# Macaron block (feed-forward, selective scan, feed-forward) on one core: the hidden units of the feed-forward kept in full precision in one buffer, and two projection weights in one buffer that is reloaded in every chunk

## The reference, cut to what matters

```python
x = L0_attn_resid                                   # (4, 1024, 512) float32
x = x + 0.5 * ffn(layernorm(x), W_up, W_gate, W_down)
x = x + attn(layernorm(x), ...)                     # a selective scan, below
x = x + 0.5 * ffn(layernorm(x), W_up, W_gate, W_down)

def ffn(x, W_up, W_gate, W_down):                   # D = 512, F = 2048
    wu, wg, wd = ternary(W_up), ternary(W_gate), ternary(W_down)   # clip(round(w / s), -1, 1) * s
    return (silu(x @ wu.T) * (x @ wg.T)) @ wd.T

def attn(r, ...):                                   # E = 1024, N = 16 states
    rn = rmsnorm(r) * norm_w
    x = silu(causal_conv4(rn @ W_in) + conv_b)
    delta = softplus(x @ W_delta_1 @ W_delta_2 + b_delta_2)
    # per position: h = h * exp(delta * A) + (delta * x) * B;  y = sum over n of h_n * C_n
    return r + ((y + x * W_D) * silu(rn @ W_skip)) @ W_out
```

## Time and profile before

| what | value |
|---|---|
| time, three runs | 2798.93, 2801.0 (median), 2805.9 us |
| span of the profiled execution, from the first to the last instruction | 2796.2 us |
| span against the median of the runs | 4.8 us less |
| busy: PE, DVE, POOL, ACT | 93%, 88%, 85%, 67% of the span |
| granted TensorE clock, mean | 0.979 of full |

### The profile page before, as it was taken

One profiled execution on the slowest core, in us unless ns is written; L12 is line 12 of the kernel. 1 busy time (PEld: TensorE's weight loads), 2 busy tenths in 40 slices (PEclk: granted clock), 3 DMA queues, 4 the chain that ended last, 5 costly groups with the idle time before them and its releaser, 6 DMA issues.

```text
span 2796.2 us, 51718 instructions
## 1 busy us (share of the span) xinstructions
PE 2614.3 (93%) x17439; PEld 2021.6 (72%) x17439; DVE 2447.7 (88%) x3221; ACT 1879.0 (67%) x4340; POOL 2382.1 (85%) x2023
## 2 busy tenths in 40 slices
PE   5776899999999999999999999999999999999878
PEld 4555677777878777786777778677777877776655
DVE  4378899999999999899999999899999999999892
ACT  7374867676676767667676766767676676767651
POOL 1168899999898999999998999999999898999881
PEclk9898999999999999999999999999999999999989
DMA  7013222223222322222232222222222222222220
GB/s 274 31 55 72 60 61 76 56 58 83 59 74 60 80 50 65 77 63 73 58 81 53 70 69 63 73 63 75 54 72 66 66 69 65 73 57 68 64 55 8
DMA packets 94446, 192.44 MB, mean 69 GB/s; under 512 B 12588, under 2 KB 32232, under 8 KB 93672
## 3 DMA queue, kind: packets, MB, share of 16 engines
q0 software_dynamic: 20304, 73.93, 13.7%
q1 hardware_dynamic: 73880, 115.21, 13.0%
HBM read 106.26 MB, written 8.91 MB: 41 GB/s over the span
## 4 chain that ended last, share of the span: by engine, by line
POOL 41%; PE 32%; issue 12%; DVE 7%; ACT 2%; DMA 1%; POOLq 1%; DVEq 0%; ACTq 0%
POOL h L778 22%; PE ps L1596 10%; POOL h L795 7%; PE ps L1607 6%; PE ps L1619 6%; POOL hl L884 4%; PE ps L1553 4%; PE ps L1668 4%; DVE h L1342 3%; POOL u L892 2%; POOL delta L849 2%; DVE xc L1400 1%; PE ps L1629 1%; POOL h L784 1%; POOL xw L799 1%
## 5 line engine op out<-in xcount | busy, mean ns | idle before, releaser
L778 POOL TENSOR_TENSOR h<-u,bb 128x1024 f32<-128x1024 f32 x512 | 1257.8, 2466 | 27.2 <-DVE u L1417 14.2
L1342 DVE TENSOR_TENSOR_SCAN h<-ps,h 128x512 f32<-128x512 f32 x1024 | 1191.8, 1207 | 36.5 <-POOL h L784 18.6
L1037 ACT ACTIVATE ps<-delta,a_neg 128x255 f32<-128x255 f32 x2048 | 873.1, 468 | 377.0 <-DVE h L1342 374.8
L1596 PE MATMUL ps<-xh,q_up 128*128 128x256 f16 x2048 | 466.5, 275 | 36.1 <-DVE xl L1280 19.1
L1364 DVE SCALAR_TENSOR_TENSOR y<-ps,ccur,y 128x512 f32<-128x512 f32 x678 | 471.4, 738 | 6.9 <-PE ps L1553 6.3
L1596 PE MATMUL ps<-xh,q_gate 128*128 128x256 f16 x2048 | 462.7, 273 | 8.1 <-DVE xw L1433 7.8
L1596 PE MATMUL ps<-xl,q_up 128*128 128x256 f16 x2048 | 466.5, 275 | 0.0
L1596 PE MATMUL ps<-xl,q_gate 128*128 128x256 f16 x2048 | 462.4, 273 | 0.0
L1553 PE MATMUL ps<-ident,h 128*128 128x128 f32 x2968 | 398.2, 277 | 50.2 <-DVE y L1364 46.7
L1553 PEld LDWEIGHTS ps<-ident,h 128*128 128x128 f32 x2968 | 344.6, 142 | 112.7 <-issue 50.9
L884 POOL TENSOR_TENSOR hl<-act,hh 128x512 f16<-128x512 f32 x256 | 314.5, 1229 | 97.3 <-ACT hh L1064 94.4
...
## 6 DMA issues: line engine op xcount, KB each, us to landing
xw<-h POOLq DMA_DIRECT2D x141, 512.0 KB, 4.5
bb<-b_scratch SPq DMA_DIRECT2D x224, 256.0 KB, 3.1
cplane<-c_scratch SPq DMA_DIRECT2D x141, 128.0 KB, 3.1
xs<-in_L_attn_resid_dram SPq DMA_DIRECT2D x17, 512.0 KB, 3.5
out_dram<-xs SPq DMA_DIRECT2D x15, 512.0 KB, 4.3
...
```

The costliest lines, as they stand in the source:

```text
L778: ins = pl.tensor_tensor(hs, u[:, :, :], bb[:, q % 2, s % PLANES:s % PLANES + 1, :].broadcast_to([P, HE, CH]), ALU.mult)
L1037: ins = ac.activation(abar[r][:, e, 1:], delta[:, k, 1:], ACT.Exp, scale=a_neg[:, k, n:n + 1])
L1342: v.tensor_tensor_scan(hr, abar[r].rearrange("p e t -> p (e t)"), hr, 0.0, ALU.mult, ALU.add).then_inc(scanned, 1)
L1596: ins = te.matmul(pp[:, f * CH:(f + 1) * CH], w[:, d, col:col + P], part[:, d, :], start=(d == 0 and part is xh), stop=(d == DB - 1 and pa ...
```

## The change

The hidden units are kept once, as float32, in `hidden` (16 blocks of 256 tokens); tanh, and the two products, are written there in place. The copy to `hh`, the subtraction into `hl` and the two-deep `act` are gone. `q_down` becomes float32, and each part of DN is one float32 matmul. The room comes from `w_in` and `w_out`, which now share `w_io`: SP loads `W_in` (2 MB) after the output projection of a chunk has ended and `W_out` (2 MB) after the input projection has, in every loop; `xn` now lies in `tmp` too. `ELEM` has eleven steps where it had nine (the last chunk seven where it had six; the first chunk nine as before). All slots but those of fill are new, and so are the lists of what comes early or late in a slot.

```diff
-qT = [..., sb("q_down", [P, FB, D], f8)]
+qT = [..., sb("q_down", [P, FB, D])]
-w_in = sb("w_in", [P, DB, E])
-w_out = sb("w_out", [P, EB, D])
+w_io = sb("w_io", [P, DB * E])
+w_in = w_io[:, :].rearrange("p (d e) -> p d e", d=DB)
+w_out = w_io[:, :].rearrange("p (e d) -> p e d", e=EB)
-act = sb("act", [P, ACTS, 2 * CH])
-hh = sb("hh", [P, FB, CH], f16)
-hl = sb("hl", [P, FB, CH], f16)
+hidden = sb("hidden", [P, FB, CH])
+xn = xr
...
 # down, on PE
-need(pe, hl_ready, PAIRS * ffn_run(ph, i, kind) + (hi + 1) // 2)
+gate, done = job_no(ph, i, f"G{kind}_{(hi - 1) // 2}")
+need(pe, bank_used[gate], done + 1)
 for f in range(lo, hi):
-    for part in (hh, hl):
-        ins = te.matmul(pp, part[:, f, t * P:(t + 1) * P], q_down[:, f, :], ...)
+    ins = te.matmul(pp, hidden[:, f, t * P:(t + 1) * P], q_down[:, f, :], ...)
...
 # removed: hidden_high on ACT (hh), hidden_low on POOL (hl)
 # tanh_up on ACT
-need(sc, hl_ready, g - ACTS + 1)
-ac.activation(act[:, p % ACTS, :], pp, ACT.Tanh, ...)
+ac.activation(hidden[:, 2 * p:2 * p + 2, :]..., pp, ACT.Tanh, ...)
...
 # normalise on ACT (xn is written into tmp)
+if kind == "n":
+    need(sc, delta_ready, 2 * i + 3)
+elif kind == "2":
+    need(sc, delta_ready, min(2 * i + 2, 2 * NCH))
 # rms_scaled on ACT: also waits for T2_0 and T2_1 on PE
...
+W_IN_AT, W_OUT_AT = 7, 10
 # SP
+def load_w_in(ph, i):
+    if ph == "fill":
+        sp.wait_ge(q_saved, ALL_SAVED)
+    else:
+        for t in range(TB):
+            bk, before = job_no(ph, i, f"OM_{t}")
+            sp.wait_ge(bank_ready[bk], before + 1)
+    sp.dma_start(w_in, W_in...).then_inc(win_loaded, 16)
+def load_w_out(ph, i):
+    for q in (3, 1):
+        bk, before = job_no(ph, i, f"IN_{q}")
+        sp.wait_ge(bank_ready[bk], before + 1)
+    sp.dma_start(w_out, W_out...).then_inc(wout_loaded, 16)
 for q in range(2, LOADS + 1):
+    if q == W_IN_AT and ph == "loop":
+        load_w_in(ph, i)
+    if q == W_OUT_AT and "IN_1" in PHASES[ph]:
+        load_w_out(ph, i)
     for s in loads_of_c(i, q):
         load_c(i, s)
     if q < LOADS:
         load_planes(i, q)
...
-ELEM = [3, 9, 11, 15, 17, 18, 22, 27, 31]
+ELEM = [3, 6, 9, 14, 15, 17, 18, 21, 22, 27, 31]
-ELEM_LAST = [5, 9, 11, 17, 23, 28]
+ELEM_LAST = [5, 10, 13, 14, 23, 26, 28]
```

More of the change, by code:

```diff
@@ L98 @@
 LOOP_SLOTS = [
[L99 to L102, removed]
+    ["T1_1", ("OM_0", 0, 4), "T1_0", "U1_0"],
+    ["G1_0"],
+    ["U1_1", "G1_1", "U1_2"],
+    ["D2_2", "G1_2", "U1_3"],
     ["D2_3", "G1_3", "YT_2"],
[L104 to L111, removed]
-    [],
[L113 to L123, removed]
+    ["YT_3", "U1_4", "G1_4", "U1_5"],
+    ["G1_5"],
+    ["U1_6", "G1_6"],
+    ["U1_7", ("OM_0", 4, 8), ("OM_1", 0, 7)],
+    ["G1_7"],
+    [],
+    [("OM_1", 7, 8), ("SK_0", 0, 2)],
+    [("DN1_0", 0, 16), ("DN1_1", 0, 2), "T2_0"],
+    [],
+    [("DN1_1", 2, 16), "T2_1"],
+    [("SK_1", 0, 2)],
+    ["U2_0", "G2_0"],
+    [("SK_2", 0, 2), ("SK_3", 0, 2), "Tp_1", "Tp_0"],
+    [("IN_2", 0, 2)],
+    ["U2_1"],
+    ["G2_1", ("IN_3", 0, 2), ("IN_0", 0, 2)],
+    ["YT_0", "YT_1", "U2_2", "G2_2"],
+    ["U2_3", ("DN2_0", 0, 2)],
+    [("IN_1", 0, 2), "G2_3", "U2_4"],
+    [("DN2_0", 2, 3), "G2_4", "U2_5"],
     ["G2_5", "DB"],
-    [("DN2_0", 5, 7), "DT", "U2_6"],
-    ["D2_0", "G2_6", "D2_1"],
-    ["U2_7", ("DN2_0", 7, 8), "G2_7"],
+    ["U2_6", "DT", ("DN2_0", 3, 8), "D2_0"],
+    ["G2_6", "D2_1"],
+    ["U2_7", "G2_7"],
     [("DN2_1", 0, 11)],
@@ L134 @@
     [],
-    ["D2_2", "U1_0"],
-    [],
+    ["D2_2"],
+    ["U1_0"],
     ["G1_0", "U1_1"],
@@ L200 @@
 DRAIN_SLOTS = [
-    [("OM_0", 0, 4)],
+    [("OM_0", 0, 1)],
+    [("OM_0", 1, 4)],
+    [],
+    [],
+    ["YT_2", ("OM_1", 0, 2)],
+    [],
+    ["YT_3", ("OM_0", 4, 5)],
     [],
@@ L606, in phases @@
             run("drain", NCH)
-        def hidden_units(ph, s):
-            return [(int(n[1]), int(n[3])) for n in ORDER[ph] if n[0] == "G" and after(ph, n, n in EARLY[ph], s)]
         @block.sync
@@ L1137, in rms_scaled @@
                 need(sc, delta_ready, 2 * i + 2)
+                if "T2_0" in PHASES[ph]:
+                    for k in range(2):
+                        bk, before = job_no(ph, i, f"T2_{k}")
+                        need(sc, bank_ready[bk], before + 1)
                 sc.sem_inc(act_go, 1)
@@ L1602, in down @@
                 bk, pp = opened(ph, i, name, lo)
-                need(pe, hl_ready, PAIRS * ffn_run(ph, i, kind) + (hi + 1) // 2)
+                gate, done = job_no(ph, i, f"G{kind}_{(hi - 1) // 2}")
+                need(pe, bank_used[gate], done + 1)
                 pe.sem_inc(pe_go, 1)
                 for f in range(lo, hi):
-                    for part in (hh, hl):
-                        ins = te.matmul(pp, part[:, f, t * P:(t + 1) * P], q_down[:, f, :],
-                                        start=(f == 0 and part is hh), stop=(f == FB - 1 and part is hl))
+                    ins = te.matmul(pp, hidden[:, f, t * P:(t + 1) * P], q_down[:, f, :], start=(f == 0), stop=(f == FB - 1))
                 if hi == FB:
@@ L1666, in out_proj @@
                 need(pe, z_ready, 4 * i - 3 + (hi - 1) // 2)
+                need(pe, wout_loaded, 16 * min(i, NCH - 1))
                 for e in range(lo, hi):
@@ L1686, in job @@
                             used(ph, i, f"Tp_{k}", name)
+                        need(pe, win_loaded, 16 * (1 + max(i, 0)))
                     project(ph, i, name, w_in, lo, hi)
```

159 lines of the change are left out of this document (67 added, 92 removed), and 3 rows, old and new, of the table BEFORE.

## The result

The changed kernel takes 3296.8 us (median of 4 runs, 3295.5 to 3297.7) against 2800.8 before: ratio 1.177, 95% interval 1.175 to 1.179. The forecast was 3195 with 3130 to 3265 as its range. The direction and the price of a down part were right, the size was 102 us short, and the range missed the time by 32 us.

What follows compares the result with a forecast made beforehand. The prediction took PE, 97% loaded, to bound the kernel, and PE alone after the change. Steady chunks +334 us and the ends made +394; 2796.2 + 394 + 4.8 = 3195 us, range 3130 to 3265.

Steps and rivals of the forecast that it cites:

- What bounds the kernel: Steady chunk before the change: PE 97% loaded, 157.7 of 162.7 us; POOL's recorded work 149.7, despite 41% of the chain.
- rival 4: POOL was the bound and its relief takes PE's idle time and the ends to their lower bounds: 3139 us, chance 10%.
- The down part: Each down projection part on PE goes from 0.432 to 0.86 us in float32, +27.4 us a chunk.
- Fill and the chunk's sum: Fill: 32 down parts in one block, +13.7 us; steady chunk: PE's load becomes 183.4 us.
- I keep 5.0: PE's idle time per steady chunk stays at 5.0 us, giving a chunk of 188.4 us.
- about 11: Upper bound in us of PE's idle time per steady chunk; the lower bound was 2.3.
- the edge at U1_0: Slot 0: U1_0 directly behind T1_0, no OM parts covering the split into xh and xl, up to 2 us.
- rival 2: Long slots starve DVE, which then bounds the short ones: 197.4 us a chunk, 3312 us in all, chance 10%.
- Two more states: Two more states by the C plane: per chunk PE loses 1.7 us, DVE loses 3.0, POOL gains 6.5.
- The reloads: Reloading w_in and w_out, 2 MB and about 9.7 us each, is covered and costs nothing.
- Rival 3: Planes queued behind the 2 MB loads hold up POOL and then the scan: 3240 us, chance 6%.
- The ends: Outside the steady stretch: fill +13.7, first +7, to the next store +9, then +14, last chunk +3, drain +13.7 us.

Runs made afterwards that it cites:

- e16: The kernel before with step 6 added to its nine C-plane steps in the loop: 2847.2 us, ratio 1.016.
- e1b: The changed kernel with the slots, early and late lists and nine C-plane steps of the kernel before: 3188.1 us, ratio 1.138.
- e2: The changed kernel with only the odd parts of the down projection multiplied, half of the hidden units left out: 2895.0 us.
- e4: The changed kernel with OM_0 parts 0 to 3 put between T1_0 and U1_0 in slot 0 of its loop: 3259.3 us.
- e7: The changed kernel with DN1 spread over slots 12 to 15 instead of 12 and 14, and IN_2, SK and U2_0 moved: 3295.1 us.
- e13: e1b with eleven C-plane steps in the loop, its nine and steps 6 and 25: 3169.3 us.
- e6: The changed kernel without the reloads of W_in and W_out from the first loop on, so with wrong input projection weights: 3296.3 us.
- e12: The changed kernel, its own slots, with the nine C-plane steps of the kernel before in the loop: 3345.6 us.

## Why the prediction was wrong

- **What bounds the kernel** was half right. PE's sum was right, and it sets the pace after the change. But the recorded 149.7 us of POOL were taken for its load; e16 shows that it had no room for step 6, and the chain's 41% for POOL was no illusion. The change relieves POOL, so this moves the forecast only by the idle time that goes with it: rival 4 gave 2.3 us a chunk in the steady stretch, and e1b, in the old slots, has 2.7. (The sum of the forecast's PE terms is 2051 / 13 = 157.8, 0.1 more than the 157.7 used.)
- **The down part**, 0.86 against 0.432: right to the hundredth. The rule of the Trainium skill ("FP8 and Floating Point Precision", TensorE Precision Notes), that true FP32 takes four passes, agrees with this trace: 4 x 0.216 = 0.86. The trace itself shows two records of 0.43 for each matmul. e2 returns 24.7 of the 27.5 us.
- **Fill and the chunk's sum**: +14.4 against 13.7, and by pitch 183.4.
- **"I keep 5.0"** is the step that failed: the idle time of PE in the new slots, a term of 5.0 us a chunk that measured 11.3. Of the 11.3, 6.9 are waits for other engines, nearly all for DVE, 2.8 are the half clock behind two of them, for which the forecast had no term, and 1.6 stand in no wait. This makes 83 of the 102 us. The same waits and the half clock, once each, are also most of what the stretch to the next store had over its term (11 us); the stretch "first" shows other waits. The upper bound of "about 11" that stood beside it was right in size. Its reason, in part, wasn't: the edge at U1_0 was named, measured at 2.06 of wait, and worth 37.5 us when taken away (e4), but was not added to the sum. That the bound fits is in part luck. The lockstep by loads per slot, on which rival 2 stood at 3312, came near the time (3296.8) by another mechanism than the one seen: e7 spreads the blocks of DN1 and gains nothing.
- **The order of the middle slots** was not followed through DVE's list at all. IN_3 and IN_0 in one slot and YT_0 and YT_1 in the next put two convs, a silu behind ACT's tanh and two additions into one series, and with four banks PE stands behind it. The slots were in the diff; the work was only counted, slot by slot, for PE.
- **Two more states** were priced at 6.5 us of POOL with cover. In e13 the two states gain 19 us, where PE's sum alone gives 24. For this choice of states, step 14 next to 15, what counted was the wait of the YT addition for the DMA: it costs 53 us on the old slots.
- **The reloads** cost nothing (e6: 3296.3), as forecast. Rival 3 is out for this kernel; a wait of that size appears in e12 only (e2 has 4.7 us in all, the other runs next to none).
- **The ends** were 21 us short in all: 0.7 in fill, 3 in first, 11 to the next store, 7 behind the steady stretch. About 3 us went the other way. The forecast added 4.8 us as what an execution has around its span; in every run with both numbers it is about 2 (3296.9 against 3295.1 here), so the profiled execution of the kernel before was most likely some 3 us faster than the median.
